# Expert rows kept as fp16 halves, with half of the row tiles transposed by DMA: a gated cross-attention and mixture-of-experts kernel on one core

## The chip, the core and the metric

The kernel runs on one core of a Trainium2 chip. The core has a matrix engine (PE, with its weight loads shown apart as PEld), a vector engine (DVE), a scalar engine (ACT), GpSimd (POOL) and SyncE (SP), and 16 DMA engines that they share. SP issues DMAs into a hardware queue (q1), POOL its indirect ones (gather, scatter with add) into a software queue (q0). The metric is the device time of one execution in microseconds, lower is better.

## What is computed

```python
x = x + tanh(g_xattn[0]) * xattn(layernorm(x), ctx, ctx, Wq, bq, ..., Wo, bo)   # heads attend to heads, token by token
x = x + tanh(g_ffn[0])   * ffn(layernorm(x), w_gate, w_shared_up, w_shared_down, w_up, w_down)

def ffn(x, ...):                        # N = 4096 tokens, C = 1024, E = 64 experts, top 6, capacity 512
    shared = (silu(g_s) * y_s) @ w_shared_down          # y_s, g_s = split(x @ w_shared_up)
    scores = sigmoid(x @ w_gate); w = top-6 scores, normalised
    x_disp[e, pos] = x[token]                           # up to 512 rows for each expert
    g_r, v_r = split(x_disp @ w_up[e])                  # 1024 -> 2 x 128
    out_r = (silu(g_r) * v_r) @ w_down[e]               # 128 -> 1024
    return shared + sum over the token's 6 experts of w * out_r
```

## The kernel before

Three phases follow one another: attention (to about 1220 us of the profile), routing with the shared expert (to about 1880 us), and the experts (the rest). Wherever fp32 accuracy is wanted, an fp32 operand is split into two fp16 halves, hi (a rounded copy) and lo (what is left), and a product is made of three fp16 matmuls, hi by hi, hi by lo and lo by hi.

**Routing** goes through the 4096 tokens in 32 tiles of 128. For each tile DVE normalises the row into `yn` (fp32), SP stores it to `rows_dram`, ACT and DVE split it into the halves `yw`, and SP turns `yw` into `yt` by one DMA transpose of 128x2048 fp16 (L1020). A POOL scatter writes each token's number and weight into the expert's list.

**Experts** are a loop over 64 experts; an expert has 512 row slots in four tiles of 128 (k = 0 to 3), two buffers by parity. All engines run one program per step e, written by hand in this order:
- POOL: `gather(e+2)`, four indirect DMAs of 128 rows of 4 KB from `rows_dram` into `rows`; then `add(e-1)`, four indirect DMAs that add the 128x1024 fp32 results `outs` into `out` in DRAM. Before the first of them it waits until the adds of the expert before have landed (the `target` list, L1551, has one buffer, as has each of the four tiles of `outs`).
- SP: `load_w(e+2)`, 1 MB of `w_up` and 0.5 MB of `w_down`, as soon as the buffer's last user, the split into lo halves of expert e, is done (L1494).
- PE: the up product of expert e in four half blocks of 12 matmuls (`up_half`), each preceded by the transposes of one tile of expert e+1 (`turn`, L1720: eight fp32 squares of 128x128 into `eturn_ps`); then the down product of expert e-1 (`down_tile`, 24 matmuls of 512 columns).
- ACT copies each turned tile out of `eturn_ps` as fp16 (`ext_hi`, L1606), DVE subtracts that copy from it (`ext_lo`, L1657), and both also split the weights, make the gate and take the down product out of PSUM into `outs`.

Nothing but program order and semaphores sets the order. In the text T(e), G(e), A(e) and W(e) stand for the transposes, gathers, adds and weight loads of expert e.

Of the kernel before, what the change touches and what calls it, by code (L numbers as in the profile page):

```python
# [22 lines left out]
F32 = mybir.dt.float32  # L23
# [8 lines left out]
P = 128  # L32
# [777 lines left out]
def routing_phase(nc, persistent, wo, x, b_o, w_gate, w_shared_up, w_shared_down, attn_dram, rows_dram,  # L810
# [3 lines left out]
    with ExitStack() as ctx:  # L814
# [149 lines left out]
        with nc.Block() as block:  # L964
            @block.sync
            def _(sp):
# [35 lines left out]
                def step(t, project, up, down):  # L1002
# [117 lines left out]
            def _(act):  # L1120
# [18 lines left out]
                def step(t, project, up_it, down_it):  # L1139
# [30 lines left out]
            def _(dve):  # L1170
# [5 lines left out]
                def norm(t):  # L1176
                    par = t.base % 2

                    dve.wait_ge(rows_stored[par], t.half().times(16))
# [218 lines left out]
def expert_phase(nc, persistent, w_up, w_down, rows_dram, table_dram, out):  # L1398
    ident, apart = persistent["ident"], persistent["apart"]
    with ExitStack() as ctx:  # L1400
# [14 lines left out]
        rows = sb("rows", [P, 2 * TPE, D], F32)  # L1415
# [7 lines left out]
        xt_hi = sb("ext_hi", [P, 2, KC, CAP], F16)  # L1423
        xt_lo = sb("ext_lo", [P, 2, KC, CAP], F16)
# [7 lines left out]
        turn_ps = ps("eturn_ps", [P, KC, P])  # L1432
# [5 lines left out]
        spare_turn_ps = down_ps[1][:].rearrange("p (k t) -> p k t", k=KC)  # L1438
# [13 lines left out]
        turned = sem("turned")  # L1452
# [13 lines left out]

        def turned_ps(e, k):
            return spare_turn_ps if e.register is None and e.base == 0 and k % 2 else turn_ps[:]
# [17 lines left out]
        with nc.Block() as block:  # L1486
            @block.sync
            def _(sp):
# [11 lines left out]

                def first():
# [3 lines left out]

                    for k in range(TPE):
                        sp.wait_ge(gathered[0][k], 16)
# [8 lines left out]
            def _(pool):  # L1516
                def gather(e):
# [6 lines left out]
                    pool.wait_ge(turned, e.times(TPE, -TPE))  # L1524
# [59 lines left out]
            def _(act):  # L1584
# [9 lines left out]

                def split_h(e):
# [5 lines left out]
                def turn(e, k):  # L1601
                    act.wait_ge(turned, e.times(TPE, k + 1))
                    if k == 0:

                        act.wait_ge(v_made, e.times(1, -1))
# [3 lines left out]
                def first():  # L1609
                    split_w(Step(0), UP)  # L1610
                    for k in range(TPE):
                        turn(Step(0), k)
# [220 lines left out]
```

## Time and profile before

| | before |
|---|---|
| median of 3 runs | 3170.62 us (3170.16 to 3171.55) |
| profiled execution, its own time | 3170.95 us |
| its span, first to last instruction | 3169.2 us |
| PE busy | 2986.0 us (94%) |
| DVE / ACT / POOL busy | 2214.7 / 1346.0 / 1372.6 us |
| DMA moved | 546.48 MB |
| mean granted clock of PE | 0.977 of full speed |

The span lies 1.75 us under the execution's own time, and that within 0.33 us of the median. The page gives the busy share of the whole; it averages three phases with different limits, so the windows of the expert loop are read by themselves. The share of the DMA engines is the time that their packets took divided by 16 engines' time, and it can pass 1 because packets in flight on one engine overlap a little.

### The profile page before, as it was taken

How to read it: one execution, taken by the hardware profiler on the slowest of the kernel's cores; microseconds unless marked ns; L12 is line 12 of the kernel's file. 1: busy time of each engine (PE TensorE's matmuls, PEld its weight loads, DVE VectorE, ACT ScalarE, POOL GpSimd, SP SyncE). 2: the span in 40 equal slices, each digit the busy share in tenths (PEclk: the TensorE clock that was granted, in tenths of full speed). 3: DMA queues.
4: the chain of work that ended last, by engine and by line, in shares of the span. 5: the costliest groups of instructions: out<-in, count | busy, mean ns of one | idle time of the engine just before them, and what ended most of it. 6: DMA issues, size and time to landing. Idle time of an engine off the chain costs nothing. (4 is left out here: it accounts for less than half of the span.)

```text
span 3169.2 us, 62918 instructions
## 1 busy us (share of the span) xinstructions
PE 2986.0 (94%) x21248; PEld 1813.3 (57%) x21248; DVE 2214.7 (70%) x3818; ACT 1346.0 (42%) x2172; POOL 1372.6 (43%) x1316
## 2 busy tenths in 40 slices
PE   5899999999999994999999969999999999999996
PEld 4677777777777762444444425555555555555552
DVE  6677777777777776777777755666666666666663
ACT  4444444444444442111111105555555555555552
POOL 1222222222222212445555544666666666666663
PEclk9999999999999996999999989999999999999998
DMA  7333334333333335444444427999999999999996
GB/s 235 78 88 84 88 88 107 98 85 87 85 87 85 87 97 177 123 140 139 134 139 133 138 80 217 269 282 278 265 275 276 264 281 280 278 286 270 284 273 138
DMA packets 433545, 546.48 MB, mean 172 GB/s; under 512 B 230391, under 2 KB 328695, under 8 KB 433376
## 3 DMA queue, kind: packets, MB, share of 16 engines
q1 hardware_dynamic: 353504, 309.12, 32.0%
q0 software_dynamic: 79872, 235.06, 31.7%
q8 instruction: 112, 1.84, 0.2%
q14 instruction: 57, 0.47, 0.1%
HBM read 340.27 MB, written 203.88 MB: 172 GB/s over the span
## 5 line engine op out<-in xcount | busy, mean ns | idle before, releaser
L1559 POOL DMA_INDIRECT out<-outs,target x256 | 402.3, 1572 | 296.2 <-ACT outs L1636 237.0
L1657 DVE TENSOR_TENSOR ext_lo<-eturn_ps,ext_hi 128x1024 f16<-128x1024 f32 x254 | 311.1, 1225 | 266.3 <-ACT ext_hi L1606 258.6
L1530 POOL DMA_INDIRECT rows<-rows_dram,index x256 | 355.2, 1388 | 120.7 <-POOL index L1526 59.4
L1606 ACT ACTIVATE ext_hi<-eturn_ps 128x1024 f16<-128x1024 f32 x254 | 260.1, 1024 | 220.6 <-PE eturn_ps L1720 164.1
L733 PE MATMUL proj_ps<-xt,wq_wo_hi 128*128 128x256 f16 x1024 | 280.5, 274 | 28.0 <-DMA xt<-xw 27.3
L1720 PE MATMUL eturn_ps<-ident,rows 128*128 128x128 f32 x2032 | 268.4, 275 | 28.5 <-DMA rows<-rows_dram,index 24.4
L733 PE MATMUL proj_ps<-ct_hi,wk_wv_hi 128*128 128x256 f16 x1024 | 280.2, 274 | 8.0 <-issue 8.0
L734 PE MATMUL proj_ps<-xt,wq_wo_hi 128*128 128x256 f16 x1024 | 280.3, 274 | 1.1 <-issue 1.1
L1720 PEld LDWEIGHTS eturn_ps<-ident,rows 128*128 128x128 f32 x2032 | 224.5, 141 | 97.6 <-DVE ext_lo L1657 50.1
L735 PE MATMUL proj_ps<-xt,wq_wo_lo 128*128 128x256 f16 x1024 | 280.2, 274 | 0.0
L734 PE MATMUL proj_ps<-ct_lo,wk_wv_hi 128*128 128x256 f16 x1024 | 280.0, 273 | 0.0
L735 PE MATMUL proj_ps<-ct_hi,wk_wv_lo 128*128 128x256 f16 x1024 | 280.0, 273 | 0.0
L1636 ACT ACTIVATE outs<-edown_ps,weight 128x512 f32<-128x512 f32 x256 | 176.0, 687 | 235.6 <-PE edown_ps L1745 222.8
L1702 DVE TENSOR_SCALAR outs<-edown_ps,weight 128x512 f32<-128x512 f32 x256 | 192.1, 751 | 115.3 <-PE edown_ps L1745 103.9
L484 ACT ACTIVATE whole<-proj_ps,bias 64x128 f32<-64x128 f32 x512 | 183.8, 359 | 187.8 <-PE proj_ps L735 183.3
L417 POOL TENSOR_TENSOR sc<-sc,neg_max 128x256 f32<-128x256 f32 x64 | 45.0, 703 | 449.0 <-DVE neg_max L626 449.0
L1081 POOL DMA_INDIRECT table_dram<-record,entry x192 | 204.2, 1063 | 76.3 <-issue 51.9
L586 DVE TENSOR_SCALAR whole<-proj_ps,bias 64x128 f32<-64x128 f32 x512 | 182.3, 356 | 69.3 <-PE proj_ps L735 57.2
L1651 DVE SCALAR_TENSOR_TENSOR ew_lo<-ew_in,ew_hi 128x2048 f16<-128x2048 f32 (+1 forms) x128 | 223.8, 1748 | 0.3 <-ACT ew_hi L1593 0.3
L749 PE MATMUL proj_ps<-wk_wv_hi,ct_hi 128*128 128x512 f16 x512 | 195.7, 382 | 12.0 <-DVE wk_wv_lo L606 12.0
L1319 PE MATMUL o_ps<-wq_wo_hi,at_hi 128*128 128x512 f16 x512 | 195.1, 381 | 11.8 <-DVE at_lo L1173 10.4
L1743 PE MATMUL edown_ps<-ew_hi,h_hi 128*128 128x512 f16 x512 | 194.7, 380 | 4.3 <-ACT outs L1636 4.3
(179 smaller groups left out, 7307.5 us busy)
## 6 DMA issues: line engine op xcount, KB each, us to landing
ew_in<-w_up SPq DMA_DIRECT2D x64, 1024.0 KB
ew_in<-w_down SPq DMA_DIRECT2D x64, 512.0 KB
x_in<-x SPq DMA_DIRECT2D x16, 1024.0 KB, 5.7
c_in<-ctx_t SPq DMA_DIRECT2D x16, 1024.0 KB, 7.9
v_dram<-vt SPq DMA_DIRECT2D x64, 256.0 KB, 2.0
late<-v_dram SPq DMA_DIRECT2D x32, 512.0 KB, 8.3
attn_dram<-attn SPq DMA_DIRECT2D x64, 256.0 KB, 2.0
a_in<-attn_dram SPq DMA_DIRECT2D x32, 512.0 KB, 4.0
```

The source lines that it names most:

```text
L733: pe.matmul(out, wh, hi[:, k, :], start=(k == 0), stop=False)
L734: pe.matmul(out, wh, lo[:, k, :], start=False, stop=False)
L735: last = pe.matmul(out, wl, hi[:, k, :], start=False, stop=(k == KC - 1))
L749: pe.matmul(proj_ps[j % BANKS][:], ch, wh, start=(k == 0), stop=False)
L1081: pool.indirect_dma_start(out=table_dram, out_offset=bass.IndirectOffsetOnAxis(ap=entry[:, par, k:k + 1], axis=0), in_=record[:, par, k, : ...
L1319: pe.matmul(to, stationary(0, c), moving(0, c), start=(c == 0), stop=False)
L1530: pool.indirect_dma_start(out=rows[:, par * TPE + k, :], out_offset=None, in_=rows_dram, in_offset=bass.IndirectOffsetOnAxis(ap=index[:, p ...
L1559: pool.indirect_dma_start(out=out, out_offset=bass.IndirectOffsetOnAxis(ap=target[:, k:k + 1], axis=0), in_=outs[:, k, :], in_offset=None, ...
L1606: act.activation(xt_hi[:, e.base % 2, :, k * P:(k + 1) * P], turned_ps(e, k), ACT.Copy).then_inc(xt_hi_made, 1)
L1651: dve.scalar_tensor_tensor(w_lo[w], w_in[w], SCALE, w_hi[w], ALU.mult, ALU.subtract).then_inc(w_lo_made[part], 1)
L1657: dve.tensor_tensor(xt_lo[:, e.base % 2, :, cols], turned_ps(e, k), xt_hi[:, e.base % 2, :, cols], ALU.subtract).then_inc(xt_lo_made, 1)
L1720: last = pe.transpose(turned_ps(e, k)[:, c, :], rows[:, par * TPE + k, c * P:(c + 1) * P], ident[:])
```

## The change

The normalised rows are kept in DRAM as their two fp16 halves side by side, 2x1024 fp16, which is the same 4 KB as before. So the gather brings halves, and no subtraction is needed behind the transposes. Of the four tiles of an expert, tiles 0 and 1 are turned by a DMA transpose each (SP, 128x2048 fp16, straight from `rows` into the stationary operand `ext`), tiles 2 and 3 by PE as 16 fp16 squares each, whose hi half ACT copies out and whose lo half DVE copies out. In routing the store of the rows waits for `yw` and is put right ahead of the routing transpose.

```diff
@@ routing, SP
                         s = t.plus(-1)
-                        sp.wait_ge(y_normed, s.times(1, 1))
-                        sp.sem_inc(apart, 1)
-                        sp.dma_start(rows_dram[bass.ds(s.times(P), P), :], yn[:, s.base % 2]
-                                     ).then_inc(rows_stored[s.base % 2], 16)
                         sp.wait_ge(y_lo_made, s.times(1, 1))
                         sp.sem_inc(apart, 1)
+                        sp.dma_start(rows_dram[bass.ds(s.times(P), P), :],
+                                     yw[:, s.base % 2].rearrange("p w d -> p (w d)")
+                                     ).then_inc(rows_stored[s.base % 2], 16)
@@ routing, ACT (the same wait leaves DVE's norm)
+                        act.wait_ge(rows_stored[t.base % 2], t.half().times(16))
                         act.activation(yw[:, t.base % 2, 0], yn[:, t.base % 2], ACT.Copy).then_inc(y_hi_made, 1)
@@ experts, tiles
-        rows = sb("rows", [P, 2 * TPE, D], F32)
+        rows = sb("rows", [P, 2 * TPE, 2 * D], F16)
-        xt_hi = sb("ext_hi", [P, 2, KC, CAP], F16)
-        xt_lo = sb("ext_lo", [P, 2, KC, CAP], F16)
+        xt = sb("ext", [P, 2, 2, KC, CAP], F16)
+        turn_ps = ps("eturn_ps", [P, 2, KC, P], F16)
@@ experts, SP
+                def turn(e, k):
+                    par = e.base % 2
+                    sp.wait_ge(gathered[par][k], e.half().times(16, 16))
+                    sp.sem_inc(apart, 1)
+                    if k == 0:
+
+                        sp.wait_ge(v_made, e.times(1, -1))
+                        sp.sem_inc(apart, 1)
+                    sp.dma_start_transpose(xt[:, par, :, :, k * P:(k + 1) * P].rearrange("p w c t -> p (w c) t"),
+                                           rows[:, par * TPE + k, :]).then_inc(turned[par][k], 16)
...
                 def step(e, up, down):
+                    if up and more(e, 1):
+                        for k in range(2):
+                            turn(e.plus(1), k)
                     if more(e, 2):
                         load_w(e.plus(2))
@@ experts, POOL gather
-                    pool.wait_ge(turned, e.times(TPE, -TPE))
+                    for k in range(2):
+                        pool.wait_ge(turned[par][k], e.half().times(16))
+                        pool.sem_inc(apart, 1)
+                    pool.wait_ge(pe_turned, e.times(2, -2))
@@ experts, ACT
                 def turn(e, k):
-                    act.wait_ge(turned, e.times(TPE, k + 1))
-                    if k == 0:
+                    act.wait_ge(pe_turned, e.times(2, k - 1))
+                    if k == 2:
                         act.wait_ge(v_made, e.times(1, -1))
-                    act.activation(xt_hi[:, e.base % 2, :, k * P:(k + 1) * P], turned_ps(e, k), ACT.Copy
+                    act.activation(xt[:, e.base % 2, 0, :, k * P:(k + 1) * P], turn_ps[:, 0], ACT.Copy
                                    ).then_inc(xt_hi_made, 1)
@@ experts, DVE
-                    dve.wait_ge(xt_hi_made, e.times(TPE, k + 1))
-                    cols = slice(k * P, (k + 1) * P)
-                    dve.tensor_tensor(xt_lo[:, e.base % 2, :, cols], turned_ps(e, k), xt_hi[:, e.base % 2, :, cols],
-                                      ALU.subtract).then_inc(xt_lo_made, 1)
+                    dve.wait_ge(pe_turned, e.times(2, k - 1))
+                    if k == 2:
+
+                        dve.wait_ge(v_made, e.times(1, -1))
+                    dve.tensor_copy(xt[:, e.base % 2, 1, :, k * P:(k + 1) * P], turn_ps[:, 1]).then_inc(xt_lo_made, 1)
@@ experts, PE
-                    for c in range(KC):
-                        last = pe.transpose(turned_ps(e, k)[:, c, :], rows[:, par * TPE + k, c * P:(c + 1) * P], ident[:])
-                    last.then_inc(turned, 1)
+                    for w in range(2):
+                        for c in range(KC):
+                            cols = slice(w * D + c * P, w * D + (c + 1) * P)
+                            last = pe.transpose(turn_ps[:, w, c, :], rows[:, par * TPE + k, cols], ident16[:])
+                    last.then_inc(pe_turned, 1)
...
+                        for k in range(2):
+                            pe.wait_ge(turned[e.base % 2][k], e.half().times(16, 16))
...
-                                if more(e, 1):
-                                    turn(e.plus(1), 2 * part + half)
+                                if more(e, 1) and half:
+                                    turn(e.plus(1), 2 + part)
                                 up_half(e, part, half)
```

SP's queue in the expert loop, two steps of it, before (`ew_in` is the weight buffer; the semaphores `e_w_lo_made0` and `1` say that the lo halves of the up and down weights are made):

```order
L1495 ISA [waits e_w_lo_made0,e_w_lo_made1]
L1495 DMA ew_in<-w_up 128x8x256
L1498 ISA
L1498 DMA ew_in<-w_down 128x1024
L1493 REGISTER_ALU
L1495 ISA [waits e_w_lo_made0,e_w_lo_made1]
L1495 DMA ew_in<-w_up 128x8x256
L1498 ISA
L1498 DMA ew_in<-w_down 128x1024
```

The first of these steps in the changed kernel (`ext` is the turned operand, `e_gathered1_0` the landing of tile 0's gather, `e_v_made` the end of an up product):

```order
L1502 ISA [waits e_gathered1_0]
L1504 DMA_TRANSPOSE ext<-rows 128x16x128 [waits e_v_made]
L1504 DMA_TRANSPOSE ext<-rows 128x16x128 [waits e_gathered1_1]
L1488 REGISTER_ALU
L1490 ISA [waits e_w_lo_made0,e_w_lo_made1]
L1490 DMA ew_in<-w_up 128x8x256
L1493 ISA
L1493 DMA ew_in<-w_down 128x1024
```

Two DMA transposes now stand in each step ahead of the next weight loads, behind two waits of their own.

PE at the start of a step of the loop before (`g_ps` takes the first half of the up product):

```order
L1755 ISA [waits e_w_lo_made0]
L1757 REGISTER_ALU [waits e_xt_lo_made]
L1715 ISA [waits e_hidden_made]
L1720 MATMUL eturn_ps<-ident,rows 128x128 [waits e_xt_lo_made,e_gathered1_0]
L1720 MATMUL eturn_ps<-ident,rows 128x128 x7
L1729 MATMUL g_ps<-ext_hi,ew_hi 128x512
L1730 MATMUL g_ps<-ext_lo,ew_hi 128x512
L1731 MATMUL g_ps<-ext_hi,ew_lo 128x512
```

And in the changed kernel, from the start of such a step to its first transposes, with the matmuls in between left out:

```order
L1773 REGISTER_ALU [waits e_turned1_1,e_turned1_0,e_w_lo_made0]
L1744 MATMUL g_ps<-ext,ew_hi 128x512 [waits e_hidden_made,e_xt_lo_made,e_xt_hi_made]
L1745 MATMUL g_ps<-ext,ew_hi 128x512
L1746 MATMUL g_ps<-ext,ew_lo 128x512
...
L1735 MATMUL eturn_ps<-ident,rows 128x128 [waits e_xt_lo_made,e_xt_hi_made,e_gathered0_2]
L1735 MATMUL eturn_ps<-ident,rows 128x128 x15
```

A step now begins with a wait for both DMA transposes (`e_turned1_0`, `e_turned1_1`) and goes straight into the up product; two groups of 16 squares take the place of four groups of 8.

## Rows read from the trace of the kernel before

**Rows 1.** The page: span, PE's share, forty slices (busy tenths, clock, DMA share).
```profile
span 3169.2 us, 62918 instructions
PE 2986.0 (94%) x21248; PEld 1813.3 (57%) x21248; DVE 2214.7 (70%) x3818; ACT 1346.0 (42%) x2172; POOL 1372.6 (43%) x1316
...
PE   5899999999999994999999969999999999999996
PEclk9999999999999996999999989999999999999998
DMA  7333334333333335444444427999999999999996
```

**Rows 2.** Windows of the expert loop; the first line names the columns.
```profile
core 0: us, PE busy (x) PEld busy (x) DVE busy (x) ACT busy (x) POOL busy (x), PEclk, DMA share, GB/s
2100.00:2400.00 300.00, 300.00 (x1637) 164.01 (x1636) 204.51 (x204) 169.91 (x191) 196.10 (x172) 1.00 1.04 274
```

**Rows 3.** DMA queues in the expert loop: packets, MB, share of 16 engines.
```profile
q0 software_dynamic: 54329, 174.74, 81.6%
q1 hardware_dynamic: 56225, 74.52, 22.8%
```

**Rows 4.** Windows with one kind of transfer each, attention phase and expert loop.
```profile
303.20:306.70 3.50, 3.50 (x48) 3.01 (x48) 3.35 (x9) 2.55 (x7) 0.00 (x0) 1.00 0.83 155
303.80:306.00 2.20, 2.20 (x23) 1.93 (x20) 2.08 (x7) 1.60 (x5) 0.00 (x0) 1.00 1.15 213
2409.60:2416.00 6.40, 6.40 (x39) 3.78 (x38) 2.75 (x3) 4.04 (x4) 4.84 (x5) 1.00 1.06 184
2403.00:2405.00 2.00, 2.00 (x11) 0.87 (x9) 1.65 (x2) 0.01 (x1) 0.73 (x3) 1.00 1.02 410
2405.00:2409.00 4.00, 4.00 (x20) 1.85 (x19) 2.85 (x5) 2.58 (x4) 1.37 (x1) 1.00 1.07 378
```

**Rows 5.** The page's DMA issues: last number is us to landing.
```profile
xt<-xw SPq DMA_TRANSPOSE x32, 4.3
```

**Rows 6.** Groups of instructions from 1900 us: busy, mean ns, idle before.
```profile
L1720 PE MATMUL eturn_ps<-ident,rows 128*128 128x128 f32 x2032 | 268.4, 275 | 28.5 <-DMA rows<-rows_dram,index 24.4 <-DVE ext_lo L1657 2.8 <-issue 1.3
L1606 ACT ACTIVATE ext_hi<-eturn_ps 128x1024 f16<-128x1024 f32 x254 | 260.1, 1024 | 220.6 <-PE eturn_ps L1720 164.1 <-issue 56.5
L1657 DVE TENSOR_TENSOR ext_lo<-eturn_ps,ext_hi 128x1024 f16<-128x1024 f32 x254 | 311.1, 1225 | 266.3 <-ACT ext_hi L1606 258.6 <-issue 4.6
```

**Rows 7.** Timeline of PE: start us, us, instruction; expert loop, then routing.
```profile
2409.55 1.04 PE L1720 MATMUL eturn_ps<-ident,rows 128*128 128x128 f32 x8
2410.43 0.38 PE L1729 MATMUL g_ps<-ext_hi,ew_hi 128*128 128x512 f16 x1
...
1519.88 0.19 PE L1381 MATMUL gate_pos_ps<-wg_hi,yt 128*128 128x64 f16 x1
1519.91 0.19 PE L1381 MATMUL gate_pos_ps<-wg_lo,yt 128*128 128x64 f16 x1
```

**Rows 8.** Timeline of SP's queue and ScalarE in one expert step.
```profile
2402.77 0.38 SPq L1495 DMA_DIRECT2D ew_in<-w_up  x1
2421.91 0.38 SPq L1495 DMA_DIRECT2D ew_in<-w_up  x1
...
2411.63 1.90 ACT L1593 ACTIVATE ew_hi<-ew_in 128x2048 f16<-128x2048 f32 x1
```

**Rows 9.** Waits from 1900 us: total us, times, longest us.
```profile
POOL target L1551 <- DMA out<-outs,target: 37.0, 27, 8.2
ACT outs L1636 <- DMA out<-outs,target: 11.8, 4, 6.0
```

**Rows 10.** Windows around a stop of PE before the routing phase.
```profile
1160.00:1165.00 5.00, 0.00 (x1) 0.00 (x1) 2.82 (x6) 4.68 (x10) 0.00 (x0) 0.70 0.34 79
1165.00:1170.00 5.00, 5.00 (x36) 2.63 (x36) 4.84 (x9) 2.84 (x4) 0.00 (x0) 0.62 0.55 197
```

**Rows 11.** Timeline of SP's queue: a routing transpose.
```profile
1509.93 2.09 SPq L1020 DMA_TRANSPOSE yt<-yw  x1
```

More of the change, by code:

```diff
@@ L1177, in norm @@
                     par = t.base % 2
-                    dve.wait_ge(rows_stored[par], t.half().times(16))
                     dve.wait_ge(y_lo_made, t.times(1, -1))
@@ L1451, in expert_phase @@
         w_lo_made = [sem(f"w_lo_made{part}") for part in (UP, DOWN)]
-        turned = sem("turned")
+        ident16_made = sem("ident16_made")
+        turned = [[sem(f"turned{i}_{k}") for k in range(2)] for i in range(2)]
+        pe_turned = sem("pe_turned")
         xt_hi_made = sem("xt_hi_made")
@@ L1616, in step @@
                     for k in range(TPE):
-                        if up and more(e, 1):
-                            turn(e.plus(1), k)
+                        if up and more(e, 1) and k % 2:
+                            turn(e.plus(1), 2 + k // 2)
                         if k == 0 and more(e, 1):
@@ L1676, in first @@
                     split_w(Step(0), UP)
-                    for k in range(TPE):
+                    for k in (2, 3):
                         turn(Step(0), k)
@@ L1682, in step @@
                     for k in range(TPE):
-                        if up and more(e, 1):
-                            turn(e.plus(1), k)
+                        if up and more(e, 1) and k % 2:
+                            turn(e.plus(1), 2 + k // 2)
                         if k == 1 and more(e, 1):
@@ L1715, in turn @@
                     pe.wait_ge(gathered[par][k], e.half().times(16, 16))
[L1717 to L1721 removed]
+                    pe.wait_ge(xt_hi_made, e.times(2, k - 2))
+                    pe.wait_ge(xt_lo_made, e.times(2, k - 2))
+                    for w in range(2):
[3 more added lines that the diff above has]
+                    last.then_inc(pe_turned, 1)
                 def up_half(e, part, half):
@@ L1728, in up_half @@
                         wh, wl = (w[:, par, at:at + HR] for w in (w_hi, w_lo))
-                        pe.matmul(out, wh, xt_hi[:, par, c, :], start=(c == 0), stop=False)
-                        pe.matmul(out, wh, xt_lo[:, par, c, :], start=False, stop=False)
-                        last = pe.matmul(out, wl, xt_hi[:, par, c, :], start=False, stop=(c == KC - 1))
+                        pe.matmul(out, wh, xt[:, par, 0, c, :], start=(c == 0), stop=False)
+                        pe.matmul(out, wh, xt[:, par, 1, c, :], start=False, stop=False)
+                        last = pe.matmul(out, wl, xt[:, par, 0, c, :], start=False, stop=(c == KC - 1))
                     if half == 1:
@@ L1748, in first @@
                 def first():
-                    for k in range(TPE):
+                    pe.wait_ge(ident16_made, 1)
+                    for k in (2, 3):
                         turn(Step(0), k)
@@ L1754, in step @@
                         pe.wait_ge(w_lo_made[UP], e.times(1, 1))
-                        pe.wait_ge(xt_lo_made, e.times(TPE, TPE))
+                        for k in range(2):
+                            pe.wait_ge(turned[e.base % 2][k], e.half().times(16, 16))
+                        pe.wait_ge(xt_hi_made, e.times(2, 2))
+                        pe.wait_ge(xt_lo_made, e.times(2, 2))
                         pe.wait_ge(hidden_made, e.times(1))
```

21 lines of the change are left out of this document (8 added, 13 removed).

## The prediction

> **What bounds the kernel now.** I read the page first, then the windows of the expert loop, then the DMA queues there. On the page [rows 1] PE looks like the bound: 94% busy, nines from end to end, the clock at full speed nearly throughout. The reader should look at the line below: the DMA engines stand at 3 to 5 tenths in attention and routing, and at 9 from the 26th slice on. The window of the loop says both things at once [rows 2]: in 300 us PE is busy for 300.00 us, and the DMA share is 1.04. One step takes 2421.91 - 2402.77 = 19.14 us, from one weight load to the next [rows 8]. The queues [rows 3] give 81.6% + 22.8% = 104.4%, so about 20.0 us of all 16 engines for every step of 19.14 us.
>
> Is 1.04 full, or is it only a large number? Windows in which one kind of transfer runs alone tell [rows 4]. Adds alone (2409.6 to 2416) stand at 1.06 and move 184 GB/s; gathers alone (2403 to 2405) at 1.02 with 410 GB/s; weight loads alone (2405 to 2409) at 1.07 with 378 GB/s. These are queues with work waiting behind them, so 1.02 to 1.07 is what full looks like. Adds are over half of the traffic's time, so a full step would show about 1.055, and 1.04 leaves some 1.5% idle, 0.3 us of a step. The waits agree: POOL waits 27 times, 37.0 us in total, for the adds of the expert before to land, and ACT for 11.8 us in 4 waits [rows 9]. So the expert loop has two bounds at the same place, PE at 19.14 us and the DMA engines at about 18.85 us. Attention and routing are nowhere near the second one.
>
> **The change part by part.**
>
> PE. Now four groups of eight fp32 squares: one group holds PE from 2409.55 to the next matmul at 2410.43, 0.88 us [rows 7], 3.5 us a step for 2032 + 16 squares in all (the 16 of the first expert go to another tile) [rows 6]. After it, two groups of 16 fp16 squares. The trace has no fp16 square transposed. The nearest rows are the gate matmuls, 128x128 fp16 weights anew for each and 64 columns, one every 0.03 us [rows 7]; 128 columns make 0.06, so 16 cost about 0.93 us and the step 1.9 us. That is 1.7 us less, PE at 17.4 us a step. The bounds: as cheap as the gate's 0.03 (1.0 us a step), or as dear as a fp32 square, 0.11 (3.5 us, no gain). In either case PE isn't above 19.14 us, so this term sets nothing once the DMA engines are over it.
>
> ACT and DVE. Four copies of 1024 ns and four subtractions of 1225 ns become two of each kind of copy [rows 6]. A plain copy from fp16 PSUM is not in the trace; between half and the whole of these durations, it frees 2 to 3 us of each engine. In 300 us DVE is busy for 204.51 us and ACT for 169.91 us [rows 2], so it is worth nothing by itself. That DVE need not wait for ACT's copy (258.6 us of idle [rows 6]) frees no one: PE does not wait long for either now.
>
> Gathers, adds, weight loads. The same bytes in the same packets: a row is still 4 KB. Nothing is saved here.
>
> DMA transposes, the term that decides. Two per step, each 128x2048 fp16, exactly the shape that attention and routing use. Such a one alone, in a stretch where nothing else moves, fills 3.5 us at a mean share of 0.83 [rows 4]: 2.9 us of 16 engines. In its middle it holds the engines at 1.15 and moves 213 GB/s, so at its own full rate it takes 2.9/1.15 = 2.5 us. Two take 5.0 us of a DMA system with 0.3 us to spare: +4.7 us a step. A DMA of this shape lands 4.3 us after its issue [rows 5], which could be hidden well (a whole step lies between issue and use); the throughput can't be.
>
> The Trainium skill (DMA: Bandwidth & Descriptors, Latency and other measured facts) gives a DMA transpose 350 to 400 GB/s if contiguous and 261 GB/s with a non-contiguous middle dimension. By the first, two would cost about 2.8 us (an estimate from that page), and the sum would be near 3320 us; by the second 4.0 us and near 3390 us. The trace shows 213 GB/s at the plateau for just this shape [rows 4], slower than either, and my sum goes by that.
>
> How many steps: the line of DMA shares has nines in slices 26 to 39 [rows 1], 14 x 79.2 us = 1109 us or 58 steps; the few ahead of them start from less load and fill their slack first. I count 60 steps in full. 60 x 4.7 = 282 us.
>
> Bounds of this term. Above: each transpose costs its 2.9 us at the mean level of the loop, 2.9/1.04 = 2.8, and there is no slack: 5.6 x 60 = 335 us. Below: an add moves 184 GB/s where a gather moves 410 at the same share, so an add leaves more than half of the data path unused, and so does a transpose (213). If the engines put the one into the other's gap, a pair costs 5.0 x 213/410 = 2.6 us, less 0.3: 2.3 x 60 = 138 us. I take the value near the top of these, because in the mixed windows of the loop the share stays at 1.04 to 1.07 with no sign of one queue's packets hiding in another's.
>
> SP's queue. The loads W(e+2) now stand behind T(e+1) and its two waits. G(e+1) was issued a step earlier and the up product of e-1 is over before step e starts, so both waits end before the lo halves of e are made and the load's own wait is still the last. From the load's issue at 2402.77 to ACT's split at 2411.63 there are 8.9 us [rows 8], of which the loads fill 4 (2405 to 2409). ACT also reaches that split about 1 us earlier, with no tile ahead of it. With transposes in the same queue and adds beside them the loads will land later than that, and ACT will wait for `ew_in` more often; where DMA is full anyway, this is one of the places where the 4.7 us shows and not an extra.
>
> Where it will show. When the DMA engines fall behind, the adds land late; POOL waits at `target`, ACT and DVE at `outs`, PE for them at `edown_ps`, or for a gather at the squares, which queue behind adds. PE then idles some 6 us of 23.8.
>
> Routing. The row store waits for `yw` and goes right ahead of the transpose. The transpose is issued at 1509.93 now [rows 11] and its result is first read at 1519.88 [rows 7]; a 0.35 us issue and 1.3 us of a store (512 KB at 410 GB/s) ahead of it, plus its 4.3 us [rows 5], leave 4 us. Cost nothing. The new wait of ACT for a store two tiles old, also nothing. Without that cover it would be 1.7 x 32 = 53 us.
>
> **Sum.** The profiled execution took 3170.95 us, 1.75 over its span and 0.33 over the median. 3170.95 + 282 = 3453, less 0.33: 3452 us.
>
> **The rivals.**
>
> (A) The DMA engines are full and the transposes add to them: 3452 us, own range 3400 to 3515. Chance 0.70.
>
> (B) The transposes hide in part in the gaps of the adds: 3170 + 138 = 3309 us, between 3200 and 3400. For it: the 184 against 410 GB/s. Against: no window shows two queues doing better together. Chance 0.15.
>
> (C) Faster. The engine time of a transpose is hidden whole, since its packets fill only gaps, and DMA stays where it is at 18.85 us while PE goes to 17.4. The step is then 18.85: -0.3 x 60 = -18 us, 3153 us; if the adds too are drawn out only by having nothing to compete with, down to PE's 17.4, 3066 us. It decides if two transposes cost under 0.3 us a step. Against it is that a single one holds all engines at 1.15 for over 2 us. Chance 0.03, and 0.02 for within 0.2%.
>
> (D) Worse than the sum. The chain through one `target` list and one `outs`, or the weight loads behind the transposes, leaves the engines idle in places though they are the bound; 2 us idle a step give 3452 + 120 = 3572 us. PE's clock belongs here: in the stop from 1160 to 1165 us, PE busy for 0.00, the granted clock fell to 0.70, and in the next 5 us, with PE busy throughout, it stood at 0.62 [rows 10]. A stop of 6 us in each step would cost PE about 2 us at the half clock (1.2 of 2.4 GHz), 17.4 + 2 = 19.4, still under 23.8 and so hidden. It decides only if the clock stays low for most of a step, when 17.4 goes to 34.8. The Trainium skill (TensorE: Matmul & The Clock Gate, HAM oscillation) describes exactly such a kernel, which stops for a DMA in every tile and goes back to the low clock in each. Chance 0.10.
>
> That the change does not do what it says can be left out: the order of instructions shows two transposes on SP and 32 squares on PE for every step.
>
> **How the numbers follow.** The time is (A)'s. The range for 8 in 10 takes (A) whole, the upper part of (B) and the lower part of (D): 3330 to 3530 us. Within 0.2% (6 us) is about what a measurement of this kernel cannot tell from no change. Faster 0.03, same 0.02, slower 0.95.
>
> **What would show it.** Right: the step at 23 to 24.5 us, DMA share still 1.04 to 1.1 in the loop, q1's share up by about 24 points of a now longer step, PE busy for 70 to 80% of it, waits on landed adds grown from 37 us to hundreds. Attention and routing unchanged within 2 us. Wrong: a DMA share well under 1 with a longer step (then it is a chain of waits, D), or a step under 21 us with a share above 1.15 (then packets overlap, B). A transposing group of 16 squares should take 0.9 us; at 1.8 us the PE term is wrong, without effect on the time.

## The result and the profile after

The changed kernel takes 3733.23 us (median of 4 runs, 3698.99 to 3740.32) beside 3171.09 us for the kernel before: ratio 1.1751, 95% interval 1.1677 to 1.1825. It is slower, as forecast, but by 562 us and not by 282, and it lies outside the range. Where the runs of a kernel lie apart, a time given below is the median of those within 1.5% of its fastest, and the span of all of them stands in brackets.

The page of the changed kernel, with the lines that answer to [rows 1]; the last one gives the chain of work that ended last, by instruction, in shares of the span:

```profile
span 3736.8 us, 63052 instructions
PE 3027.1 (81%) x21248; PEld 1748.9 (47%) x21248; DVE 1996.5 (53%) x3690; ACT 1210.0 (32%) x2045; POOL 1351.3 (36%) x1316
...
PE   5999999999997799999946678667666578668765
PEclk9999999999998899999977888788788788889887
DMA  6233343333323544544479999999999999999998
...
SPq L1504 26%; DMA ew_in<-w_up 6%; DMA rows<-rows_dram,index 4%; SPq L1493 1%; PE eturn_ps L1735 1%; SPq L1490 1%; POOL out L1570 1%; PE edown_ps L1760 1%; PE edown_ps L1758 1%; PE edown_ps L1759 1%; PE v_ps L1744 1%; PE v_ps L1745 1%; PE v_ps L1746 1%; DMA ext<-rows 0%; PE g_ps L1744 0%
```

All of the loss is in the expert loop: from slice 21 on PE falls to 4 to 8 tenths, while the DMA engines stand at 9. The chain that ended last runs for 26% of the span through L1504, SP's DMA transpose. The windows of the loop, beside [rows 2]:

```profile
core 0: us, PE busy (x) PEld busy (x) DVE busy (x) ACT busy (x) POOL busy (x), PEclk, DMA share, GB/s
2100.00:2400.00 300.00, 219.02 (x1144) 104.02 (x1144) 105.71 (x121) 94.07 (x110) 137.29 (x124) 0.84 1.10 231
2100.00:3000.00 900.00, 621.51 (x3216) 294.31 (x3217) 296.18 (x338) 264.02 (x308) 372.81 (x341) 0.83 1.11 218
```

The share rose from 1.04 to 1.10, and the bytes moved each microsecond fell from 274 to 231. That pair is the finding: the engines hold more packets and move less. The waits from 2300 to 3500 us (total us, times, longest); the two of [rows 9] grew from 37.0 and 11.8 us, nine- and nineteenfold:

```profile
ACT ew_hi L1604 <- DMA ew_in<-w_up: 423.6, 36, 23.0
POOL target L1562 <- DMA out<-outs,target: 347.2, 41, 26.8
...
ACT outs L1648 <- DMA out<-outs,target: 224.9, 50, 23.1
...
PE g_ps L1744 <- DMA ext<-rows: 157.4, 23, 10.9
```

The windows are not even. Here are five of 4 us in one step:

```profile
2542.00:2546.00 4.00, 4.00 (x20) 1.86 (x19) 2.79 (x4) 1.54 (x4) 3.19 (x2) 1.00 1.01 293
2546.00:2550.00 4.00, 4.00 (x32) 2.27 (x30) 1.93 (x2) 2.80 (x2) 3.40 (x3) 1.00 1.55 126
2550.00:2554.00 4.00, 4.00 (x32) 2.32 (x31) 2.88 (x3) 1.54 (x2) 2.76 (x3) 1.00 1.68 41
2554.00:2558.00 4.00, 4.00 (x21) 1.81 (x19) 1.38 (x2) 1.02 (x1) 2.58 (x4) 1.00 0.48 94
2558.00:2562.00 4.00, 2.75 (x12) 0.90 (x10) 0.75 (x1) 1.20 (x2) 0.00 (x0) 1.00 1.05 196
```

At a share of 1.68 the engines move 41 GB/s. They have packets in flight and PE is still busy, so it is no want of work that slows them. I call this a slow stretch. From 2000 to 3000 us the bytes moved lie under 120 GB/s for 178 us in all, in stretches of up to 27 us; in e8 below such stretches of 4 us and more are gone. The queues in it (2550 to 2555) and in another (2780 to 2798): packets, MB, share of 16 engines.

```profile
q0 software_dynamic: 43, 0.17, 128.6%
q1 hardware_dynamic: 32, 0.01, 7.4%
...
q1 hardware_dynamic: 1464, 0.37, 106.1%
q0 software_dynamic: 200, 0.67, 21.6%
```

In the first, 1.286 x 5 us x 16 / 43 = 2.4 us for each add packet of 4 KB, 0.33 us elsewhere; in the second, 1.061 x 18 x 16 / 1464 = 0.21 us for each transposing packet of 256 bytes, 0.018 us elsewhere. What packets take beyond their usual time is mostly that of the transposing ones: from 2000 to 3000 us one of them takes 42.3 ns in the mean, in e8 below 18.3 ns, which for the 4096 of a step on 16 engines is 10.8 against 4.7 us, while a packet of GpSimd's rows takes 287 against 271 ns in the mean. SP's queue shows the steps:

```profile
2493.95 21.37 SPq L1504 DMA_TRANSPOSE ext<-rows  x2
2515.72 0.39 SPq L1490 DMA_DIRECT2D ew_in<-w_up  x1
2516.31 0.78 SPq L1493 DMA_DIRECT2D ew_in<-w_down  x1
2517.70 20.76 SPq L1504 DMA_TRANSPOSE ext<-rows  x2
2538.87 0.40 SPq L1490 DMA_DIRECT2D ew_in<-w_up  x1
2539.49 0.41 SPq L1493 DMA_DIRECT2D ew_in<-w_down  x1
2540.15 29.48 SPq L1504 DMA_TRANSPOSE ext<-rows  x2
```

Between 2000 and 3600 us two of these loads lie 27.96 us apart in the mean over 55 steps, but the median is 25.1, and a quarter of the steps takes under 22.4 us, ten of them under 19: some steps are as forecast or shorter, 15 of them are over 30 us, the longest 59.4.

### The profile page after: what moved, and what is told of

Same layout as the page of the kernel before. It is cut to its first block and busy times, and to the rows that moved or that the text cites. A ratio compares the mean times of both kernels' runs of the same rounds, so it can differ in the third digit from the quotient of the medians.

```text
span 3736.8 us, 63052 instructions
## 1 busy us (share of the span) xinstructions
PE 3027.1 (81%) x21248; PEld 1748.9 (47%) x21248; DVE 1996.5 (53%) x3690; ACT 1210.0 (32%) x2045; POOL 1351.3 (36%) x1316
## 5 line engine op out<-in xcount | busy, mean ns | idle before, releaser
L1744 PE MATMUL g_ps<-ext,ew_hi 128*128 128x512 f16 x512 | 225.6, 441 | 248.9 <-DMA ext<-rows 247.8
L1604 ACT ACTIVATE ew_hi<-ew_in 128x2048 f16<-128x2048 f32 (+1 forms) x128 | 189.5, 1480 | 596.8 <-DMA ew_in<-w_up 596.7
L1671 DVE COPY ext<-eturn_ps 128x1024 f16<-128x1024 f16 x128 | 88.2, 689 | 496.3 <-PE eturn_ps L1735 496.2
L1758 PE MATMUL edown_ps<-ew_hi,h_hi 128*128 128x512 f16 x512 | 205.1, 400 | 158.9 <-ACT outs L1648 158.9
L1541 POOL DMA_INDIRECT rows<-rows_dram,index x256 | 284.1, 1110 | 120.3 <-POOL index L1537 58.9
L1735 PE MATMUL eturn_ps<-ident,rows 128*128 128x128 f16 x2048 | 155.2, 236 | 150.6 <-ACT ext L1611 104.6
L1735 PEld LDWEIGHTS eturn_ps<-ident,rows 128*128 128x128 f16 x2048 | 140.8, 107 | 193.7 <-ACT ext L1611 116.0
L1745 PE MATMUL g_ps<-ext,ew_hi 128*128 128x512 f16 x512 | 224.5, 438 | 0.0
L1746 PE MATMUL g_ps<-ext,ew_lo 128*128 128x512 f16 x512 | 222.8, 435 | 0.0
```

Source lines behind the costliest of these rows:

```text
L1541: pool.indirect_dma_start(out=rows[:, par * TPE + k, :], out_offset=None, in_=rows_dram, in_offset=bass.IndirectOffsetOnAxis(ap=index[:, p ...
L1735: last = pe.transpose(turn_ps[:, w, c, :], rows[:, par * TPE + k, cols], ident16[:])
L1744: pe.matmul(out, wh, xt[:, par, 0, c, :], start=(c == 0), stop=False)
L1745: pe.matmul(out, wh, xt[:, par, 1, c, :], start=False, stop=False)
L1746: last = pe.matmul(out, wl, xt[:, par, 0, c, :], start=False, stop=(c == KC - 1))
L1758: pe.matmul(to, hh, w_hi[:, par, cols], start=True, stop=False)
```

## The experiments

"Work" below is a count over the packets' records from 2000 to 3000 us: each packet counts with the time that its kind takes where it runs alone, brought to a share of 1, and the sum is divided by 16 engines' time, in half microseconds sorted by what is in flight. Full is about 1.0. T+Q0 are the half microseconds that hold packets of a transpose and rows of GpSimd's queue, and no weight load of SP's. The levels hang on the times that are put in: with plain packet times (18 ns for a transposing packet, 46 for a load, 159 for a gather, 328 for an add) the work in T+Q0 is 0.66 in the changed kernel, 0.54 in e2, 0.62 in e6, 0.56 in e12 and 0.85 in e16, where the text below has 0.61, 0.50, 0.58, 0.52 and 0.78.

**Parts of the change, one by one.** e1: halves, and all four tiles turned by PE.

```diff
-                    for k in range(2):
+                    for k in range(0):
                         turn(Step(0), k)
```

> Undoes the DMA transposes alone: rows stay fp16 halves, all four tiles are turned by PE in 16 fp16 squares each. PE's step is then 72 x 0.217 + 4 x 0.93 = 19.3 us against 19.14. Every theory that puts the whole loss on the DMA transposes expects 3165 to 3190 us. If a part of the loss comes from the halves themselves (the row store behind the split, the fp16 copies, one buffer for the turned tiles), it stays here: over 3200 us.

Measured 3171.93 us against 3169.16, ratio 1.0008 (0.9998 to 1.0018). Halves in DRAM, fp16 squares, plain copies and the moved store cost nothing; the whole loss is in the DMA transposes. e3 leaves them out and puts nothing in their place:

```diff
-                        for k in range(2):
+                        for k in range(0):
                             turn(e.plus(1), k)
```

> The changed kernel without its DMA transposes: tiles 0 and 1 are not turned at all (that half of the operand stays zero, so this work is left out). PE's step is 17.4 us. If the DMA engines are the second bound at about 18.85 us, as the prediction has it, the time is about 3153 us, with waits on DMA in place of PE's nines. If they are not and the share of 1.04 only looks full, it is 3066 us. No theory expects over 3175 us.

3136.02 us, 0.9904 (0.9886 to 0.9923); two of the four tiles of an expert are not turned in it at all. PE has room in it, and the windows from 2100 to 2400 us say who has none:

```profile
2100.00:2400.00 300.00, 285.67 (x1687) 144.15 (x1686) 159.22 (x180) 141.32 (x165) 213.67 (x178) 0.98 1.05 281
```

A step is 18.48 us in the mean and 17.7 in the median, where PE alone would take 17.4. So there is a second bound near the first, as predicted, but it lies a little under the 18.85 us that the prediction gave it. e4 silences the adds, so that the experts' results don't reach `out`:

```diff
-  in_=outs[:, k, :], in_offset=None, bounds_check=N + CAP - 1, oob_is_err=True,
+  in_=outs[:, k, :], in_offset=None, bounds_check=0, oob_is_err=False,
```

> The changed kernel with its scattered adds left out (all targets but row 0 lie out of bounds and are skipped, so the routed results don't arrive). If the stretches of the changed kernel in which packets take several times their usual time come from adds and transposes in flight together, they are gone here: transposing packets at 18 ns nearly throughout, no 2 us under a tenth of the usual bytes, PE the bound at 17.4 us, about 3065 us. If gathers or weight loads are enough for them, the holes stay and the time is over 3150 us. If the long issue of the transposes on SP's queue (20 us for two) is a property of the queue and not of the adds, SP's step stays over 20 us and the time over 3220 us.

3115.36 us, 0.983 (0.981 to 0.985): with the transposes but without the adds the kernel is faster than before. It lies between the two times that were expected. Gathers and loads beside a transpose lengthen its packets too, but less: 26 ns in the mean, and 1.4% of them over 150 ns, against 6.8% in the changed kernel. So the large loss of this kernel needs the adds; that they do it by themselves is not shown.

**One transpose instead of two** (e2, the other three tiles on PE):

```diff
-                        for k in range(2):
+                        for k in range(1):
                             turn(e.plus(1), k)
```

> One tile of an expert by DMA transpose instead of two, three by PE: the dose halved. By the sum (2.5 us of DMA engines for each transpose, 0.3 us to spare) the time is 3170 + 60 x 2.2 = 3302 us. If the stretches in which almost nothing moves come with transposes in flight beside adds and gathers, they are there too, but fewer or shorter: 3302 plus about half of the 260 us that they took, 3430 us. If SP's queue is the cause (loads behind a blocked transpose), one transpose blocks it for under 10 us of a step and costs nothing of its own: 3302 us or less.

3754.95 us (3733 to 4020), 1.1844 (1.1774 to 1.1914). Half of the transposed bytes costs at least as much as all of them (the changed kernel's runs are 3699 to 3740 us, 1.1677 to 1.1825), where the sum gave 3302 and a loss in proportion 3430. A price for each transpose can't give that. In T+Q0 the work is 0.50 (450 us), in the changed kernel 0.61 (457 us).

**Is it a queue or a dependence?** e6 takes the weight loads from behind the transposes in SP's queue and lets ACT issue them.

```diff
@@ SP, step
-                    if more(e, 2):
-                        load_w(e.plus(2))
@@ ACT, step, ahead of the split of the weights
+                    if more(e, 2):
+                        load_w(e.plus(2))
```

> The changed kernel with the weight loads of the loop issued by ACT's queue instead of SP's, so that they no longer stand behind transposes that hold the queue for 20 us of a step. If the loss over the sum is the late weight loads (ACT waited 423.6 us for them in the 1200 us from 2300 to 3500), the time falls to about the sum, 3450 us. If the engines are the bound and the rest is stretches with few bytes moved, the wait moves elsewhere and the time stays between 3650 and 3760 us.

4231.72 us (to 4548 in the other three runs), worse than either expectation. Freed from SP, the loads run beside transposes too, the time in T+Q0, which holds the loads of ACT's queue here, rises to 829 us at a work of 0.58 (counted with the half microseconds that hold a load, the changed kernel has 538 us), and the loop gets worse. So late loads are not what has to be mended first; since the edit also makes more of the mixture, it says nothing on what they cost by themselves. e7 adds two transposes of a constant tile to the kernel before, on which nothing waits but their own buffer:

```diff
+                        for i in range(2):
+                            sp.wait_ge(moved[i], e.times(16))
+                            sp.dma_start_transpose(unused[:, i], still[:]).then_inc(moved[i], 16)
```

> The kernel before, plus two DMA transposes of 128x2048 fp16 in each expert step on SP's queue, from a constant tile into tiles that nobody reads: their load on the DMA engines without any data dependence, nothing removed elsewhere. If the loss is the DMA engines' time and the disturbance that transposes bring to other transfers, it is all here: 3650 to 3780 us. If the loss over the sum is the chain that the change has made (gather, transpose, PE), this one stops at the sum, about 3450 us.

3790.57 us (3767 to 3870), 1.1956 (1.1881 to 1.2032). The traffic makes the loss; no reader of the turned tiles is needed for it. The weight loads still stand behind the transposes in SP's queue here.

**Keeping them apart.** In e5 SP waits, ahead of T, for all adds issued, and POOL, ahead of A, for both transposes. Gathers may still meet a transpose.

```diff
+                        for j in range(TPE):
+                            sp.wait_ge(rows_added[j], e.times(16, -32))
...
+                        for j in range(2):
+                            pool.wait_ge(turned[e.base % 2][j], e.plus(2).half().times(16, 16))
```

> Adds and transposes never in flight together: the transposes of expert e+1 wait until the adds of e-2 have landed, and the adds of e-1 until those transposes have landed. If the part of the loss over the predicted sum (about 280 us) is the price of mixing the two kinds, the stretches with almost no bytes moved are gone and the time comes back to about the sum, 3430 to 3530 us, in spite of two new waits of some 2 us in each step. If it is instead a chain of waits through SP's queue, the stricter order makes it longer: over 3730 us.

3544.8 us, 1.1172 (1.1139 to 1.1205): two sets of waits more, 188 us less. T+Q0 falls from 457 to 122 us. e8 has SP wait for the gathers too, so that nothing of GpSimd's queue is ever beside a transpose:

```diff
+                            for j in range(TPE):
+                                sp.wait_ge(gathered[nxt.base % 2][j], nxt.half().times(16, 16))
```

> As the kernel that kept adds and transposes apart (3544.8 us, in which slow stretches remained while gathers and transposes were in flight together), and now the transposes of e+1 also wait until the gather of e+2 has landed, so nothing of GpSimd's queue is in flight beside a transpose. If any transfer of that queue beside a transpose makes the slow stretches, they are now gone entirely and two transposes take 5 us: 3450 to 3550 us, bubbles included. If they don't come from the mixture, they stay, and the extra wait makes the time longer than 3545 us by 60 us or more.

3626.55 us, 1.1439 (1.1422 to 1.1455). No slow stretch is left, no transposing packet over 0.2 us, and the steps are even (24.8 to 28.6 us, mean 26.67). A stretch with a transpose alone and PE idle, then the loop:

```profile
2448.00:2451.00 3.00, 0.00 (x0) 0.00 (x0) 0.00 (x0) 0.00 (x0) 0.00 (x0) 0.75 0.98 216
...
2100.00:3000.00 900.00, 657.37 (x3506) 312.39 (x3507) 327.44 (x369) 293.01 (x335) 428.02 (x371) 0.86 0.93 236
```

This is the cleanest measure of the term. Packets take 26.67 x 0.93 = 24.8 us of a step, before they took 19.14 x 1.04 = 19.9: two transposes are 4.9 us of 16 engines, and 5.0 was forecast. Their own packets are 4.7 us of it. Now the engines stand empty for a while at each change of hands, which is why e8 is slower than e5. In the changed kernel packets take 27.96 x 1.11 = 31.0 us of a step for the same bytes, 6.2 us more than in e8.

e17 is e8 with the adds of empty slots skipped and e11 is the kernel before with that edit alone.

```diff
-  in_=outs[:, k, :], in_offset=None, bounds_check=N + CAP - 1, oob_is_err=True,
+  in_=outs[:, k, :], in_offset=None, bounds_check=N - 1, oob_is_err=False,
```

> The kernel that keeps transposes wholly apart (3626.6 us, a step of 26.5 us with no slow stretch), with the adds of empty slots skipped. There the DMA engines' work is one after the other, so 2.4 us of adds less are 2.4 us of a step less: 3627 - 60 x 2.4 = 3483 us. If something else than the engines' work sets that step, it gains under 1 us a step: over 3565 us.

> The kernel before, with the adds of empty slots skipped (119 of 512 rows of an expert on average carry no token; their targets lie past the last token and are now out of bounds). This takes 119 x 328 ns / 16 = 2.4 us of the DMA engines' time off each step. If PE alone bounds the kernel before, nothing changes in the loop and only the last adds end sooner: 3160 to 3172 us. If the DMA engines hold it up as well, up to 0.5 us a step: 3140 us.

e17: 3572.68 us, 1.127 (1.1251 to 1.1289). e11: 3160.64 us (10 runs) against 3169.57, ratio 0.9969 (0.996 to 0.9979), with the share at 0.94 and PE at 300.00 of 300. Room on the DMA engines was worth 0.9 us a step in the kernel that keeps the transposes apart, where 2.4 was expected if the engines' work set the step, and 9 us in all in the kernel before. So the step of e8 and e17 (share 0.93 and 0.89) is set by the order of the waits and not by the engines' work; its 4.9 us above is a count of packet time, not of step time. e11, slightly faster than both kernels, is the version to keep.

**What sets a slow stretch off?** I first held that it takes adds that arrive in the middle of a transpose. e12 has only POOL wait (adds never start during T), e13 only SP, e14 has neither adds nor gathers start during T, though those in flight go on.

```diff
@@ POOL ahead of the adds (e12, e14)
+                        for j in range(2):
+                            pool.wait_ge(turned[e.base % 2][j], e.plus(2).half().times(16, 16))
@@ SP ahead of the transposes (e13)
+                        for j in range(TPE):
+                            sp.wait_ge(rows_added[j], e.times(16, -32))
@@ POOL ahead of the gathers (e14)
+                        for k in range(2):
+                            pool.wait_ge(turned[nxt.base % 2][k], nxt.half().times(16, 16))
```

> Only one half of the separation: the adds of e-1 wait until the transposes of e+1 have landed; the transposes may still start amid adds. In the changed kernel's trace the slow stretches (transposing packets at about 340 ns, 6 adds a us where 48 are usual) mostly begin when packets of GpSimd's queue arrive on a transpose that already runs alone, while transposes that start amid running adds go at 32 ns with 48 adds a us beside them. If arrival is what starts a stretch, this kernel has few of them, left over from gathers: 3450 to 3580 us. If being in flight together is enough, in either order, it stays near 3730 us.

> The other half: the transposes of e+1 wait until the adds of e-2 have landed; the adds of e-1 may arrive while they run. If arrival is what starts a stretch, this makes it worse, since every transpose now starts by itself and is arrived upon: over 3750 us. If any mixture counts, the mixed time is shorter than in the changed kernel and it gets faster: 3550 to 3700 us.

> Adds and gathers both wait until the transposes ahead of them have landed, so nothing of GpSimd's queue arrives on a running transpose, while transposes may still start amid adds. By the arrival theory no stretch is left, the engines are full at the sum of their work, 23.6 to 24.5 us a step: 3440 to 3510 us, less than the 3545 and 3627 us of the two kernels that kept them wholly apart. By the theory that every mixture costs, it lies over 3545 us.

e12: 4048.52 us (4020 to 4145), about 1.28 times the kernel before, the work 0.52 over 654 us. e13: 3656.51 us, 1.1558 (1.1504 to 1.1612). e14: 3747.42 us (3737 to 3798), about 1.18 times, no better than the change. That theory fell: what goes with the time is not who arrives, but for how long both are in flight. Counted with the half microseconds that hold a load too, the time from 2000 to 3000 us with a transpose beside GpSimd's rows is 122 us in e5, 309 in e13, 530 in e14, 538 in the changed kernel, 614 in e2, 629 in e7, 728 in e12 and 829 in e6. The profiled executions follow in the same order: 3549, 3632, 3737, 3739, 3777, 3870, 4020 and 4232 us; e8, with 0 us and its empty gaps, takes 3629. A slow stretch is itself time with both in flight, so this order alone doesn't say which makes which. That e5 and e8, whose waits keep the two apart, have less of one and lose less by it, does.

e16 issues each transpose as two halves, one after the other has landed:

```diff
-                    sp.dma_start_transpose(xt[:, par, :, :, k * P:(k + 1) * P].rearrange("p w c t -> p (w c) t"),
-                                           rows[:, par * TPE + k, :]).then_inc(turned[par][k], 16)
+                    for w in range(2):
+                        if w:
+                            sp.wait_ge(turned[par][k], e.half().times(32, 16))
...
+                        sp.dma_start_transpose(xt[:, par, w, :, k * P:(k + 1) * P],
+                                               rows[:, par * TPE + k, w * D:(w + 1) * D]).then_inc(turned[par][k], 16)
```

> The changed kernel with each transpose issued as two of half the size (the hi half, then the lo half), each issued only when the one ahead of it has landed, so that at most 1024 of the 4096 packets of a step are outstanding. If the backlog on SP's queue makes the slow stretches, they go, and the time falls to 3450 to 3600 us. If it is the mixture, the transposes are drawn out over more of the step, more of it is mixed, and the time rises: 3750 to 4100 us.

3742.19 us, 1.1791 (1.1755 to 1.1828). The mixture does better, 0.78, but two more landings are waited for, and the time stays where it was. Neither expectation came out whole, and why smaller transposes mix better is open.

**Does it need GpSimd's queue?** e15 silences gathers and adds and lets ACT issue the loads.

```diff
-                            bounds_check=N - 1, oob_is_err=False).then_inc(gathered[par][k], 16)
+                            bounds_check=0, oob_is_err=False).then_inc(gathered[par][k], 16)
```

> Transposes beside weight loads alone: the kernel whose loads ACT issues (4424 us), with adds and gathers left out but for one row each (the experts then work on zeros), so that the loads of ACT's hardware queue are nearly all that runs beside the transposes of SP's. PE is the bound, about 3060 us, so the time tells little; what is read is the share of half microseconds with both kinds in flight and their work. If any second queue beside a transpose slows both, their work there is 0.5 to 0.65 of the usual, and a transposing packet often takes over 100 ns. If it needs GpSimd's queue, it is 0.9 or more.

3041.05 us, one run, no slow stretch of 4 us or more; but loads and transposes were in flight together for 57 us of 1000 only, so it decides little. e18 and e19 silence the same and copy 4 MB in each step, issued by ACT or by POOL.

```diff
+                        act.wait_ge(copied, e.times(16))
+                        act.dma_start(spare[0:8 * P, :], x[0:8 * P, :]).then_inc(copied, 16)
```

> What is left out: the gathers move no row after the first and the adds add none (their index bound is 0), so the output is not the reference's; in their place ScalarE's own queue copies 4 MB of x to a spare tensor in each step, rows of 4 KB, no faster than one copy after another. The two transposes and the weight loads stay. Theory A, any other queue beside a transpose makes the slow stretches: half-microseconds with packets of both in flight do 0.5 to 0.65 of their nominal work, and many transposing packets take over 300 ns, as in the changed kernel. Theory B, it takes the rows that GpSimd's queue moves: the transposing packets stay at 18 to 35 ns, with hardly any over 150 ns, and the stretches do 0.85 to 1.0. The total time says little, since other work is moved: 3150 to 3500 us in either.

> The same with the same left out, except that GpSimd's queue issues the 4 MB of copies. Theory A expects what it expects of the twin. Theory B expects the slow stretches here and not in the twin: 0.5 to 0.65 of the nominal work where both are in flight, and 5 per cent or more of the transposing packets over 300 ns. If neither shows slow stretches, it takes the scattered rows, gathered or added, and not the queue that issues them.

e18 took 4474.11 us and e19 3617.51, one run each. Windows of e18, and its queues from 2110 to 2120 us (q10 is ACT's):

```profile
2100.00:2110.00 10.00, 0.00 (x0) 0.00 (x0) 0.00 (x0) 0.00 (x0) 0.00 (x0) 0.50 1.30 149
2110.00:2120.00 10.00, 0.00 (x0) 0.00 (x0) 0.00 (x0) 0.00 (x0) 0.00 (x0) 0.50 1.31 40
2120.00:2130.00 10.00, 0.00 (x0) 0.00 (x0) 0.00 (x0) 0.00 (x0) 0.00 (x0) 0.50 1.66 79
```

```profile
q1 hardware_dynamic: 282, 0.07, 65.1%
q0 software_dynamic: 266, 0.00, 47.0%
q10 hardware_dynamic: 9, 0.33, 19.4%
```

The share is far over 1 with 40 to 149 GB/s: slow stretches without one row of GpSimd's queue (its packets here carry no row, 4 or 8 bytes each). Counted in windows of 2.5 us, because a packet of these copies is 64 KB and takes 2.43 us, the work of transposes beside copies is 0.31 in e18 (740 us) and 0.44 in e19 (365 us), below what theory A said. Theory B fell: no row of GpSimd's queue is needed. The copies' packets are 16 times as long as a row, so the two runs don't tell what small packets of another queue would do, and GpSimd's own packets without a row, and SP's loads, are in flight in them too.

## Why the prediction was wrong

**The step that failed** is the cost of the transposes, "I take the value near the top of these, because in the mixed windows of the loop the share stays at 1.04 to 1.07 with no sign of one queue's packets hiding in another's", with its upper bound "each transpose costs its 2.9 us at the mean level of the loop". Those windows mixed gathers, adds and loads, never a transpose, so the overlap of a transpose with another queue was put at nothing lost, without a row that shows it. I asked whether a mixture could do better than its parts and left out that it could do worse. It does: 4.9 us a step are the transposes themselves (e8), 6.2 us more are packets that stay in flight longer in the mixture, nearly all of them transposing ones. The work counted as lost in mixed half microseconds, 176 us in 1000, is 5 us of a step of 28. The sum with it is near the result, 60 x (4.9 + 5 - 0.3) = 576 us against 562; this is my reckoning after the fact. No edit removes the mixing without adding waits, so what it costs is bounded from below by e5 (188 us less) and not measured by itself.

**Rival (A)** had the transposes' load on the DMA engines, and the size of its term, right, not the whole price: in T+Q0 the engines' packets fill their time and do 0.61 of the work. **Rival (B)** is out: on balance nothing hides. **Rival (C)** is out by e8. **Rival (D)** came nearest by its time, 3572, and its reasons are not the main cause: in e5 and e8 the loads stand behind the transposes in SP's order as before, `target` and `outs` have one buffer as before, there are more waits, and both kernels are faster. Its mark, "a DMA share well under 1 with a longer step", did not appear either; the share is 1.11. What late loads and late adds take in the changed kernel beyond that was not measured by itself.

**PE** as forecast. A group of 16 fp16 squares, answering to [rows 7]:

```profile
2767.72 1.06 PE L1735 MATMUL eturn_ps<-ident,rows 128*128 128x128 f16 x16
2768.61 0.38 PE L1744 MATMUL v_ps<-ext,ew_hi 128*128 128x512 f16 x1
```

From its start to the next matmul 0.89 us, 0.93 forecast. PE's clock cost what was said: in the loop it was granted 0.83 in the mean, PE was busy for 621.51 / 900 x 27.96 = 19.3 us of a step where I had 17.4, and that stays hidden under 27.96. The Trainium skill (TensorE: Matmul & The Clock Gate, HAM oscillation) describes a kernel that stops for a DMA and falls to the low clock; the trace agrees, with 0.84 here beside 1.00 before. After PE stood still from 2565 to 2570 us (busy 0.00 of 5 us), it was granted 0.50, the lower of its two levels, in the next 5 us. By the sum above this has no price here.

**DMA rate** of a transpose: 216 GB/s alone in e8, beside 213 in [rows 4]. The Trainium skill (DMA: Bandwidth & Descriptors, Latency and other measured facts) has 261 to 400 GB/s; the measurement decides.

**Attention and routing** as forecast, unchanged: from 100 to 1150 us PE is busy for 1026.89 us, before 1028.64, and from 1220 to 1880 us for 629.90 us, before 630.79.

**Waits** went where they were expected, adds and `ew_in`; only that SP would stand 6 to 44 us at a pair of transposes (21 in the median), against 2.09 us for one before [rows 11], was not foreseen. It comes with the mixture and is not the price of issuing them: in e7 it is there too (8 to 57 us), and in e8 every pair takes 3.4 to 4.1 us, as here:

```profile
2021.77 3.45 SPq L1512 DMA_TRANSPOSE ext<-rows  x2
```

## What to carry to other kernels

Before a DMA transpose goes into a loop whose DMA engines are loaded, ask which other queue will be in flight beside it and for how long; price the transpose by its own engine time only where it runs alone. A share above 1 with fewer GB/s than any kind moves alone (adds 184, transposes 213, gathers 410 here) is how the trouble looks in windows, and it doesn't show in waits, which blame whichever transfer lands late. If PE can turn a loop's rows in the time that it has, as here (e1, ratio 1.0008), leave them there.

## What was not expected of the hardware

- Transposes in flight beside GpSimd's gathers and adds, or beside large copies of ACT's or GpSimd's queue, make slow stretches, up to 27 us in the changed kernel, at 41 GB/s with a share of 1.68 in the one shown, and less transposed data (e2) doesn't mean fewer. In them a transposing packet, 18 ns when all is well, takes about as long as a packet of the other queue: of 142150 in the changed kernel 4281 took 300 to 400 ns (an add's packet takes 328), and in e18 843 of 99568 took 2.4 to 2.5 us (a copy's takes 2.43). It looks as if packets of the two took turns on an engine; no run tests that, and it doesn't explain why adds themselves take 2.4 us there. What sets a stretch off and what ends it stays open.
- Adds of 4 KB rows cost an engine 328 ns, gathers of the same rows 159 ns, and skipping those that go to empty slots brings the share from 1.04 to 0.94 (e11) but 9 us only, since PE is the other bound.
- Two kernels with the same bytes differ by some 500 us (e5 and e12) by which of two queues waits for which.
